# Moving the maxima's row DMAs from ScalarE's queue to SyncE's, and reordering the small tasks of a fused attention and mixture-of-experts kernel

## The reference, cut to what matters

```python
x = L0_attn_x                                  # (32, 256, 128)
xn = _layernorm(x)
x = x + attn(xn) + ffn(xn)
# attn: q, k, v = heads(xn @ W + b); probs = softmax(mask(q @ k.T / sqrt(8))); (probs @ v) @ Wm + bm
# ffn:  x = xn + attention(rmsnorm(xn))        # latent keys and values, rotary embedding, 16 heads
#       xn2 = rmsnorm(x)
#       shared = experts(xn2, sWg, sWu, sWd);  logits = xn2 @ Wgate + expert_bias
#       routed = sum over the top 2 of 8 experts of comb * (silu(xn2 @ Wg) * (xn2 @ Wu)) @ Wd
#       return x + shared + routed
```

## Time and profile before

| what | value |
|---|---|
| median of 3 runs (range) | 1547.73 us (1546.21 to 1547.84) |
| the profiled execution's own time | 1547.35 us |
| its span, first to last instruction | 1545.6 us |
| mean granted TensorE clock | 0.936 |
| PE, DVE, ACT, POOL busy | 1360.3, 1116.2, 978.2, 717.3 us |

### The profile page before, as it was taken

How to read it: one execution, slowest core, us unless ns; L and a number is a source line. 1 busy time by engine, 2 the same in 40 slices (tenths; PEclk the granted TensorE clock), 3 DMA queues, 4 the chain that set the end, 5 groups by cost and what they waited for, 6 DMA issues and landing times.

```text
span 1545.6 us, 38750 instructions
## 1 busy us (share of the span) xinstructions
PE 1360.3 (88%) x15462; PEld 954.7 (62%) x15462; DVE 1116.2 (72%) x2293; ACT 978.2 (63%) x1583; POOL 717.3 (46%) x804
## 2 busy tenths in 40 slices
PE   4578899999998989989999989999999999999876
PEld 3345566666666666666666666666666666666644
DVE  6566687877868787777877778787878778687523
ACT  1046666677676667667676767677666666666672
POOL 5243445545444555534445553545455444445112
PEclk9979899999999999899898999989898999999888
DMA  5745554445555544545554454545544455544100
GB/s 131 139 95 113 115 118 105 102 91 106 106 110 122 114 103 102 104 92 107 115 121 102 105 107 90 109 105 123 114 106 106 77 111 107 117 110 102 28 2 14
DMA packets 145877, 156.29 MB, mean 101 GB/s; under 512 B 38592, under 2 KB 132452, under 8 KB 139556
## 3 DMA queue, kind: packets, MB, share of 16 engines
q1 hardware_dynamic: 126244, 152.24, 46.0%
q10 hardware_dynamic: 19456, 1.59, 1.4%
HBM read 83.03 MB, written 67.11 MB: 97 GB/s over the span
## 4 chain that ended last, share of the span: by engine, by line
PE 69%; ACT 13%; DVE 5%; ACTq 5%; issue 4%; SPq 1%; DMA 1%; POOL 1%; POOLq 0%; DVEq 0%
PE ps L221 21%; PE psm L221 14%; PE pse L221 14%; PE psv L221 13%; ACT PT L1128 6%; ACT pse L1134 5%; ACTq L1167 5%; PE ps L353 3%; DVE R L766 1%; ACT OT L1144 1%; PE ps L419 1%; DVE xs L706 1%; PE ps L344 1%; SPq L1481 1%; ACT th L1178 1%
## 5 line engine op out<-in xcount | busy, mean ns | idle before, releaser
L766 DVE TRANSPOSE_TENSOR_REDUCE R<-psm 128x32 f32<-128x1024 f32 x384 | 478.1, 1245 | 273.0 <-PE psm L221 271.5
L1128 ACT ACTIVATE PT<-pse 128x1024 f32<-128x1024 f32 x384 | 392.9, 1023 | 253.5 <-PE pse L221 251.4
L1134 ACT ACTIVATE pse<-maskb 128x512 f32<-128x512 bf16 x510 | 285.5, 592 | 86.7 <-issue 75.8
L221 PE MATMUL pse<-qsB,ks 128*128 128x512 f32 (+1 forms) x768 | 236.7, 445 | 56.2 <-ACT pse L1134 56.2
L221 PEld LDWEIGHTS pse<-qsB,ks 128*128 128x128 f32 (+1 forms) x768 | 112.2, 206 | 106.8 <-issue 77.7
L221 PE MATMUL psm<-qsB,ksm 128*128 128x256 f32 (+1 forms) x640 | 144.1, 341 | 35.1 <-DVE R L766 21.5
L1298 POOL TENSOR_TENSOR sm<-sm,half 128x2 f32<-128x2 f32 x32 | 22.9, 717 | 289.1 <-DVE sm L681 289.0
L221 PEld LDWEIGHTS psm<-qsB,ksm 128*128 128x128 f32 x640 | 101.4, 204 | 54.1 <-DVE R L766 36.4
L1385 POOL TENSOR_TENSOR hT<-th,cbs 128x512 f32<-128x512 f32 x64 | 81.8, 1279 | 113.4 <-DVE th L889 56.8
L1334 POOL TENSOR_TENSOR tc_<-tc_,ts_ 128x512 f32<-128x512 f32 x64 | 81.7, 1276 | 73.8 <-DVE ts_ L732 73.7
L1144 ACT ACTIVATE OT<-psv 128x512 f32<-128x512 f32 x128 | 75.8, 592 | 62.7 <-PE psv L221 62.6
(11 more groups left out here) (195 smaller groups left out, 2708.4 us busy)
## 6 DMA issues: line engine op xcount, KB each, us to landing
scrB<-pB SPq DMA_DIRECT2D x32, 1536.0 KB, 6.0
qsB<-scrB SPq DMA_DIRECT2D x384, 128.0 KB
scrA<-pA SPq DMA_DIRECT2D x128, 96.0 KB, 2.3
qsA<-scrA SPq DMA_DIRECT2D x124, 64.0 KB
ksA<-scrA SPq DMA_DIRECT2D x124, 64.0 KB
qsA<-scrA SPq DMA_DIRECT2D x132, 32.0 KB
ksA<-scrA SPq DMA_DIRECT2D x132, 32.0 KB
xs<-in_x SPq DMA_DIRECT2D x16, 256.0 KB, 2.9
```

The lines of the kernel that those rows point to most:

```text
L221: return e.matmul(o, l, r, start=start, stop=stop, skip_group_check=True)
L766: e.tensor_reduce(red, MX[:].rearrange("p i (c q) -> p (i c) q", q=32), AX.X, ALU.max, apply_transpose=True).then_inc(s_mr, 1)
L1128: e.activation(PT[g % 4], EX[:], ACT.Exp, scale=(8.0 ** -0.5, 0.125)[br]).then_inc(s_pt, 1)
L1134: e.activation(EX[:, i].rearrange("p (h q) -> p h q", h=4), bc(maskb[:], 4), ACT.Copy).then_inc(s_sd, 1)
```

## The change

`max_row` and its DMAs leave ScalarE and stand in SP's list: branch 1's in slot 0 and branch 0's in slot 6. Branch 0's row goes out as one DMA for both halves of 64 partitions, two DMAs in place of four; the semaphore values that wait for it are halved to match. Beside this, the lists of all engines are rewritten.

```diff
-                w.wait_ge(d_c[0], 64 * (b + 1))
+                w.wait_ge(d_c[0], 32 * (b + 1))
...
-                        exp_unit(br, c, u, (1, c) if k == 2 else (0, n1) if k == 7 and n1 < NB else None)
+                        exp_unit(br, c, u)
...
-                if row:
-                    max_row(*row)
...
+            def max_row(br, b):
+                s = b % 2
+                w.wait_ge(s_cc, 2 * b + br + 1)
+                if b >= 2:
+                    w.wait_ge(s_ex, unit(br, b - 2, 5) + 1)
+                for r in range(2):
+                    if br == 0:
+                        dst = qsA[s][48 + r:113 + r:64].rearrange("i h (b c) -> i (h b) c", c=32)
+                        e.dma_start(dst, cA[:, r]).then_inc(d_c[0], 16)
+                    else:
+                        dst = qsB[s][112 + r:113 + r].bitcast(F32).rearrange("o h (b c) -> o (h b) c", c=32)
+                        e.dma_start(dst, cB[:, r].bitcast(F32)).then_inc(d_c[1], 16)
...
+                    if k == 0:
+                        if even and done:
+                            store(p - 1)
+                        if body:
+                            max_row(1, c)
+                    if k == 1 and soon:
                         stack_a(n2)
+                    if k == 6 and n1 < NB:
+                        max_row(0, n1)
+                    if k == 9 and soon:
+                        stacks_b(n2)
                     if k == 6 and even and c // 2 + 2 < NB // 2:
                         load_x(c // 2 + 2)
```

More of the change, by code:

```diff
@@ L544, in _ @@
                     br, u = divmod(k, 6)
-                    if k == 0 and before:
-                        pv_half(1, c - 1, 1)
+                    if k == 0:
+                        if odd and moe:
+                            moe_u(p, 1)
+                            moe_c(p)
+                        if even and done:
+                            moe_d(p - 1, (4, 0))
+                        if before:
+                            pv_half(1, c - 1, 1)
                     if k == 1:
@@ L595, in _ @@
                     now += 0.5
[L596 to L602, removed]
+                    if k == 0:
+                        if body:
+                            join_max(1, c)
+                        if soon:
+                            prep_x(n2)
@@ L603, in _ @@
+                    if k == 1 and even and done:
+                        moe_d(p - 1, (2, 3))
+                    if k == 2 and soon:
+                        prep_qk(n2)
+                    if k == 3 and n1 < NB:
+                        prep_k2(n1)
+                    if k == 4:
+                        if body:
+                            norm(0, c, 0)
+                        if soon:
+                            prep_v(n2)
+                    if k == 5:
                         if odd and moe:
-                            moe_g(p, 4)
@@ L605, in _ @@
-                    if k == 2:
-                        if even and done:
-                            moe_t(p - 1)
+                            moe_sel(p, 0)
                         if soon:
[L609 to L612, removed]
+                            prep_rope(n2, 0)
+                    if k == 6:
                         if n1 < NB:
[L614 to L618, removed]
@@ L636, in _ @@
                             norm(0, c, 1)
[L637 to L641, removed]
-                        if even and moe:
[L643 to L657, removed]
+                        if even and moe:
+                            moe_gate(p)
+                    if k == 10 and odd and moe:
+                        moe_u(p, 2)
+                        moe_u(p, 3)
+                    if k == 11 and odd and moe:
+                        moe_sel(p, 3)
         @block.vector
@@ L997, in _ @@
                     br, u = divmod(k, 6)
[L998 to L1008, removed]
-                        if soon:
-                            prep_blo(n2)
-                        if body:
-                            norm(0, c, 0)
+                    if k == 0:
+                        if odd and moe:
+                            moe_hu(p, 1)
+                        if soon3:
+                            stats(n2 + 1)
@@ new lines, in _ @@
+                    if k == 1:
+                        if body:
+                            max_row(1, c)
+                        if before:
+                            norm(1, c - 1, 1)
+                        if soon:
+                            prep_xlo(n2)
+                    if k == 3:
+                        if odd and moe:
+                            moe_hg(p, 4)
+                        if even and done:
+                            moe_out(p - 1)
+                        if soon3:
+                            stats2(n2 + 1)
+                        if before:
+                            tail(c - 1)
@@ L1453, in _ @@
                             prep_n(n2 + 1)
+                        if odd and moe:
+                            moe_h(p, 3)
+                        if before:
+                            tail(c - 1)
+                    if k == 11 and soon:
+                        prep_kt(n2)
         @block.sync
```

275 lines of the change are left out of this document (129 added, 146 removed).

## The result

The changed kernel takes 1492.95 us (median of 4 runs, 1483.66 to 1498.86), the kernel before 1546.97 us in the same measurement: a ratio of 0.9653, 95% interval 0.9589 to 0.9718. The profiled execution took 1483.66 us, so what its rows show is the fast end of a kernel whose runs spread over 1%.

The account below looks back on a forecast made before the run. TensorE was taken to be held by ScalarE's row DMA issues ahead of the mask, with clock falls behind that wait. Terms of -3.6, -5.1, +2.4, +1.7 and +0.5 gave -4.1 us per pair, times 16 -66: 1481 us, range 1455 to 1515.

Parts of the forecast that it names:

- the likeliest case: The forecast itself, 1481 us with DVE and SP somewhat late: chance 0.50, range 1455 to 1515 us.
- row DMAs off ScalarE: TensorE's slot 8 waits for the mask, stretched scores and a DVE wait go: -3.6 us per pair, bounds -2.7 and -4.0.
- clock, both terms: Half-speed time behind slot 8's wait goes, -5.1 us per pair; new falls behind DVE's lateness cost +1.7.
- DVE late: DVE finishes slot 0's reduction late, so TensorE waits ahead of slot 1's scores: +2.4 us per pair, bounds 0 and 4.5.
- SP, reads and row late: `scrB`'s write waits behind `load_x`, so slot 6 of odd iterations gets `qsB` late: +0.5 us per pair, bounds 0 and 2.6.
- The detail on `cA`: In odd iterations DVE's small cast `cA` gets free of POOL, removing 0.33 us of TensorE's wait in slot 8.
- DVE neither kept up: Rival: DVE's gaps hide and the clock stays full, 1416 us, up to 1455; chance 0.22.
- its upper bound: Rival: one more DVE lock wait per pair and twice the clock loss, 1543 us; chance 0.16.
- The late-landing rival: `qsB` reads and branch 1's row land late, slot 6 of odd iterations waits 2.6 us, clock falls: 1570 us; slower 0.08.
- Its mark of 4.6 us: The late-landing rival decides when slot 6's wait and its clock cost pass 4.6 us per pair.
- The case that the change does little: Rival: the DMA issues would be hidden behind something else, result within 0.2%; chance 0.04.
- One sign of being wrong: In the profile after, a wait of TensorE for a DMA in slot 6 above 1 us would speak against the forecast.

Follow-up runs that it names:

- e1: The kernel before, with only the rows of the maxima issued from SP, branch 0's as one DMA for both halves: 1480.95 us, ratio 0.9588.
- e8: The kernel before, with branch 0's row merged into two DMAs but still issued from ScalarE: 1495.64 us, ratio 0.9683.
- e9: e1 with `moe_exp` ahead of `prep_rot` on ScalarE in slot 8 of even iterations: 1440.81 us, ratio 0.9328.
- e11: e1 with DVE taking `stats2` in slot 3 and not in slot 8: 1472.28 us, ratio 0.9527.
- e3: The changed kernel, with `load_x` on SP between the write of `scrB` and the reads of `qsB`: 1459.42 us, ratio 0.9446.
- e7: The changed kernel, with `tail` ahead of `prep_n` again on GpSimd: 1467.06 us, ratio 0.9499.
- e4: The changed kernel, with DVE taking `stats` in slot 2 again, as before the change: 1500.39 us, ratio 0.9713.
- e5: The changed kernel with the edits of e3 and e4 together: 1422.84 us, ratio 0.9218.
- e10: e5 with `moe_route5` ahead of the normalisation of slot 11 on DVE: 1420.11 us, ratio 0.9192.

## Why the prediction was right, and where its sizes were off

The forecast was 1481 us and the median is 1493, inside its own range of 1455 to 1515; the likeliest case is the one that happened, DVE and SP late where TensorE had been held by ScalarE. Term by term, per pair of iterations (means over iterations 4 to 29):

| term | forecast | measured |
|---|---|---|
| row DMAs off ScalarE | -3.6 | -3.8 |
| clock, both terms | -3.4 | -3.0 |
| DVE late | +2.4 | +2.2 |
| SP, reads and row late | +0.5 | +1.6 |
| other waits, even slot 10 above all | none | -0.7 |
| sum (before rounding) | -4.1 | -3.8 |

The profiled execution is one of the quick ones. Its span is 63.7 us shorter than that of before, 4.0 per pair; by the medians it is 54 us, 3.4 per pair. That is why the sum agrees better than the median does. There is luck in it as well: SP's term came out 1.1 too small, and most of that was made up by 0.7 that no term had, chiefly the 0.48 us that TensorE had waited for `R` in even slot 10.

*Row DMAs.* TensorE's idle time in slot 8 fell from 3.23 us per pair to nothing, and the 0.6 of stretched scores went with it. e1 and e8 show that this is a matter of issue time alone. The 0.33 us of odd slot 8 went too, but e1 keeps 0.31 of it, so that part belongs to the order. The detail on `cA` held for odd iterations: beside the earlier trace rows, its cast is now free in 18 of 32 blocks; in the other 14, all in even iterations, GpSimd's `th` (L1359) holds it. `cB`'s cast is held in 28 of 32.

```profile
L782 DVE CAST cA<-negm x32: 181/182/764, 71.4 to 1387.0; 128x32 bf16<-128x32 f32 x32
L782 DVE CAST cB<-negm x32: 181/402/645, 92.4 to 1408.7; 128x32 fp32r<-128x32 f32 x32
```

*The clock.* The forecast took off 5.1 and put 1.7 back. In these iterations the price had been 4.71, not 5.1, and 1.70 came back. That the 1.7 was hit is luck: it was charged for falls behind DVE's waits. Of the eleven falls in these iterations only five came behind slot 1, 0.66 us per pair; the other six, 1.05 us, came at slot 6's wait for the reads. With its clock DVE's lateness cost 2.9 us where 4.1 were forecast, and SP's 2.6 where 0.5 was.

*DVE.* The place was right in the main: the waits in slot 1 of odd iterations rose from 0.70 to 2.14 us (0.66 for `R`, 1.48 for `BT`), slot 0 from nothing to 0.57 (`moe_route5`'s last step, which I had not named) and even slot 11 to 0.19. Even slot 10, where more waiting was forecast, lost what it had. DVE's hold moved as forecast: in after L841, beside `pB`, takes 1570 ns at the median against 193 at best, and L825 (before's L827), beside `x2lo`, 1299 against 255. The Trainium skill, in SBUF — State Buffer, section "SBUF: two separate sides", has the shared pair locked for a whole instruction; e9 and e11 agree, since steps that met `pB` at different points took different times and all ended within 0.05 us of its end (L829 2.98 us, L833 2.77, L843 1.10).

*SP, the term that was mis-sized.* "The reads start 6.4 us late against TensorE" and "+0.5; bounds 0 and 2.6". The mechanism is the forecast one (e3, e7), and the size was +1.6, that is 1.74 us of waiting in slot 6 of odd iterations (less 0.2 for the mask that had been there), with 1.05 of the clock on top, which I had not charged to it. The sub-step that failed is the landing of the write. I took the 6.0 us of the earlier trace rows, but the write is now issued 0.5 us behind `load_x`'s 256 KB. In iteration 16 it went out at 809.39 and the reads started at 816.17, 6.8 us later; in iteration 14 it was 7.9. In all twelve even iterations that have a load (4 to 26) the write landed in 6.7 to 8.1 us. Over all blocks, with a load ahead or without, after has for L1481:

```profile
DMA to landing us min/median/max: 5.9/6.5/8.1
```

In e3, where the write goes ahead of the load, it lands as before:

```profile
DMA to landing us min/median/max: 5.9/6.0/8.3
```

In iteration 14 slot 11's exponential starts at 723.93, as soon as its scores are done, and the reads at 732.57, 8.6 us behind, where I had 6.4. Nearly 2 us of this were covered by DVE's own lateness, as forecast, and e4 shows the cover: without it the wait is 3.93 us. I had no row of two DMAs close behind each other on SP and should have taken the 8.1 at the top of the earlier trace rows as the upper bound in this term.

*The rivals.* DVE neither kept up nor reached its upper bound. The late-landing rival (slower, 1570) named the right place, and a fall behind it. Its mark of 4.6 us of wait and clock per pair was put too low: its own sum replaces the 1.7 of the forecast, and by that sum the mark is 6.3. In after the wait of 1.74 us and the falls at it, 1.05, make 2.8. e4 is this rival with the cover taken away, at 3.93 us of wait and 2.5 of clock. It passes the mark and is still 3% below before, because slot 1's 1.43 us of waiting, which that sum still counts in DVE's +2.4, went with the cover, and no other fall is left. Nothing in any run speaks for the part of it that put branch 1's row behind the reads: among TensorE's waits none is for a row DMA. The case that the change does little is excluded by the interval.

*The signs.* ScalarE's queue left the chain, the mask follows the exponential, slot 8's wait is gone, and the write of `scrB` goes out 5.5 us behind `pB`, all as written down. A mean clock above 0.95 holds in two of the four runs. The waits for `R` came up in even slot 11 and odd slot 1 only. One sign of being wrong came true: TensorE's wait for a DMA in slot 6 is above 1 us, 1.74 on average and up to 3.69. It points at SP's term, the one that was too small.

What stays open: why after's own runs spread over 1% (1483.66 to 1498.86) while e3's and e5's spread over 0.3%. The clock alone does not explain it: the runs of 1483.66 and 1498.02 us had nearly the same granted clock, 0.965 and 0.964. In after TensorE meets the reads' landing within a few microseconds, and the landing of the write varies by 1.4 us, so a varying wait in slot 6 is a candidate; no run shows it.

## What to carry to other kernels

A DMA issue is work of the engine that makes it: look for it between two instructions that the bottleneck engine waits for, and merge it or give it to SP. When one wait goes, the next one is already waiting behind it; fix the later of two waits in a row first, since the earlier one is its cover, and taking that one away alone brought nothing here (1500 us against 1493), while behind the other edit it brought 37 us. In a queue that works in order, don't put a task that waits for a late engine ahead of a transfer that somebody needs.

## What the runs showed of the hardware

The clock paid more than the waits. Between before and after, TensorE's idle time differs by 0.21 us per pair and the clock's price by 3.01. e10 still idles for 3.45 us per pair, in waits of 0.71 us at most, and lost no clock in iterations 4 to 29. One wait was dearer than two of the same sum: e4's of 3.93 us in slot 6 went with 2.5 us of clock per pair while TensorE was busy, after's, 2.14 us in slot 1 and 1.74 in slot 6, with 1.7.

A VectorE step on 128 x 32 numbers that takes 0.19 us alone took up to 3.0 us beside one GpSimd instruction of 2.4 us, more than the length of that instruction. It started at 710.94, while the one ahead of that (`kt_`, to 711.54) was still running, and ended with `pB`; I read this as held by both.
